# Squares as the stationary operand, byte-sign sums on VectorE and a polynomial inverse, in a macaron block on one core

## What is computed

```python
def ffn(x):                       # W_fc 512x128, W_proj 128x512
    y = square(relu(x @ W_fc.T)) @ W_proj.T
    mem = 0
    for _ in range(5):            # one input y, five steps
        reset = mem - 1 > 0
        mem = 0.9 * mem + y - reset
        spikes += mem - 1 > 0
    return spikes / 5
def attention(h):                 # per batch, down the 512 tokens
    keys, values = h @ Wk.T + bk, h @ Wv.T + bv
    w = exp((keys @ Wka.T + bka) / sqrt(128))
    w = w / cumsum(w, axis=1)
    return cumsum(w * keys, axis=1) * values
x = x + 0.5 * ffn(layernorm(x))
x = x + attention(layernorm(x) * gamma + beta)
x = x + 0.5 * ffn(layernorm(x))
```

## Time and profile before

| | us |
|---|---|
| median of 3 runs (156.86 to 157.18) | 157.02 |
| the profiled execution | 156.96 |
| its span, first to last instruction | 155.2 |
| PE matmul busy | 149.2 (96%) |
| DVE busy | 135.0 (87%) |
| ACT busy | 122.2 (79%) |
| POOL busy | 108.8 (70%) |

### The profile page before, as it was taken

The page is one execution under the profiler, slowest core; times in us unless marked ns, Lnnn a source line. Parts: engine busy times, 40 slices in busy tenths (PEclk is TensorE's granted clock), DMA queues, the critical chain, the costliest instruction groups (busy, mean ns, idle before and its releaser), DMA issues.

```text
span 155.2 us, 2591 instructions
## 1 busy us (share of the span) xinstructions
PE 149.2 (96%) x771; PEld 103.6 (67%) x771; DVE 135.0 (87%) x395; ACT 122.2 (79%) x238; POOL 108.8 (70%) x166
## 2 busy tenths in 40 slices
PE   6899999999999999999999999999999999999990
PEld 6684847585757848678566685785876848664790
DVE  2894589897999999999999999999999999965774
ACT  3286989899996985968989779498597685989871
POOL 1339128989699876899899999999987659080200
PEclk9999999999999999999999999999999999999999
DMA  4874000000000000000000020000020200211222
GB/s 158 231 196 143 0 2 4 0 0 2 0 2 4 2 0 0 0 4 0 0 0 0 0 72 2 0 0 0 2 72 0 68 0 1 67 44 30 68 68 70
DMA packets 10383, 5.08 MB, mean 33 GB/s; under 512 B 1153, under 2 KB 10241, under 8 KB 10369
## 3 DMA queue, kind: packets, MB, share of 16 engines
q1 hardware_dynamic: 9696, 4.40, 9.8%
q10 hardware_dynamic: 672, 0.52, 1.0%
HBM read 2.82 MB, written 2.10 MB: 32 GB/s over the span
## 4 chain that ended last, share of the span: by engine, by line
PE 93%; DVE 2%; DMA 2%; ACT 0%; issue 0%; SPq 0%; ACTq 0%
PE work L860 33%; PE hidden L796 10%; PE hidden L800 10%; PE hidden L797 9%; PE hidden L900 7%; PE work L809 5%; PE att_work L796 2%; PE att_work L800 2%; PE att_work L797 2%; PE att_work L909 2%; PE att_value L933 2%; DMA x_first<-_attn_hidden_states_dram 2%; PE att_value L796 1%; PE att_value L800 1%; PE att_value L797 1%; PE work L870 1%
## 5 line engine op out<-in xcount | busy, mean ns | idle before, releaser
L860 PE MATMUL work<-square,proj_t 128*128 128x512 f32 x120 | 58.0, 595 | 0.0
L415 ACT ACTIVATE relu<-hidden 128x512 f32<-128x512 f32 x64 | 39.7, 622 | 12.3 <-PE hidden L800 12.2
L448 ACT ACTIVATE signs<-work 128x512 bf16<-128x512 f32 x70 | 41.4, 612 | 7.2 <-PE work L860 7.2
L420 ACT ACTIVATE square<-relu 128x512 f32<-128x512 f32 x45 | 29.6, 657 | 0.6
L860 PEld LDWEIGHTS work<-square,proj_t 128*128 128x128 f32 x120 | 20.3, 189 | 12.7 <-issue 6.0
L672 DVE RECIPROCAL inv_sum<-weight_sum 128x256 f32<-128x256 f32 x16 | 27.9, 1741 | 0.0
L796 PE MATMUL hidden<-in_hi,fc_lo 128*128 128x512 f32 x64 | 27.1, 423 | 0.0
L343 POOL TENSOR_TENSOR rstd<-var_eps,minus_half 128x4 f32<-128x4 f32 x15 | 16.2, 1080 | 13.3 <-DVE neg_mean L529 13.3
L800 PE MATMUL hidden<-in_lo,fc_hi 128*128 128x512 f32 x64 | 25.2, 393 | 0.0
L797 PE MATMUL hidden<-in_hi,fc_hi 128*128 128x512 f32 x64 | 25.1, 392 | 0.0
L349 POOL TENSOR_SCALAR normed_att<-x_att,neg_mean_att,rstd_att 128x128 f32<-128x128 f32 x32 | 18.8, 600 | 0.8
(11 more groups left out here) (118 smaller groups left out, 265.5 us busy)
## 6 DMA issues: line engine op xcount, KB each, us to landing
x_first<-_attn_hidden_states_dram SPq DMA_DIRECT2D x7, 256.0 KB, 3.3
out_dram<-x_out SPq DMA_DIRECT2D x7, 256.0 KB, 2.2
fc_raw<-in_L_ffn_W_fc_dram ACTq DMA_DIRECT2D x1, 256.0 KB, 3.3
x_first<-_attn_hidden_states_dram SPq DMA_DIRECT2D x4, 64.0 KB, 3.0
proj_raw<-in_L_ffn_W_proj_dram ACTq DMA_DIRECT2D x1, 256.0 KB, 3.6
out_dram<-x_out SPq DMA_DIRECT2D x4, 64.0 KB, 1.5
att_raw<-in_L_attn_Wk_dram SPq DMA_DIRECT2D x1, 64.0 KB, 2.8
att_raw<-in_L_attn_Wv_dram SPq DMA_DIRECT2D x1, 64.0 KB, 2.5
```

The costliest lines, as they stand in the source:

```text
L415: nc.scalar.activation(relu[j.lane][:, c, :], hidden[c][:], ACT.Relu).then_inc(relu_made[j.lane], 1)
L420: nc.scalar.activation(square[j.lane][:, c, :], relu[j.lane][:, c, :], ACT.Square).then_inc(squares_act[j.lane], 1)
L448: nc.scalar.activation(signs[j.lane][:, k, :], work[j.lane][:], ACT.Sign, bias=bias, scale=scale).then_inc(signs_made[j.lane], 1)
L860: mm = nc.tensor.matmul(work[j.lane][:], proj_t[:, c, :], square[j.lane][:, c, :], start=(c == CONTRACT_ORDER[0]), stop=(c == CONTRACT_ORD ...
```

## The change

- **Contraction.** Every job is contracted as the last one was: for each chunk, four matmuls with a 128x128 tile of squares stationary and 128 columns of `proj_t` moving, into the same bank. The result has tokens on partitions. The counts (L900), their semaphore and the bf16 identity go.
- **Signs.** ACT writes the signs as bytes (0 or 1), for every job. DVE adds the planes by four adds over 256 words of 16 bits, now for attention jobs too, and the job's add reads the byte sum from SBUF.
- **Inverse.** In place of the reciprocal: ACT takes `guess` = exp(scale x bits + bias) of the running sum read as an integer, an estimate of its inverse. POOL multiplies `guess_sum` = sum x guess and `guess_share` = weight_key x guess. The rest is a cubic in guess_sum, as a linear factor by a quadratic one: ACT squares guess_sum off its centre into a PSUM bank `share_bank`, DVE adds `REST` and multiplies by guess_share (`att_near_share`), then multiplies by guess_sum - ROOT (`att_share_key`), both in that bank, and the scan reads it there. `weight_key` = (key + bias) x weight is made by DVE from `att_work`; ACT's key goes.
- **Banks.** `hidden` has three banks in rotation, and the one set free is `share_bank`.
- **Squares.** POOL squares no chunk of attention jobs; ACT does all four.
- **Layer norm.** `neg_mean` goes; the normalisation subtracts the mean from `moments`.
- **Order.** All four engines' lists are rearranged; the values are made in step i+1, the weight scan in step i.

```diff
-POOL_SQUARES = [(0,), (0,)]
-SIGN_ADDS = [4, 0]
 LAST_SQUARES = {"pool": (0,), "dve": (1, 2), "act": (3,)}
+POOL_SQUARES = [(0,), ()]
+SIGN_ADDS = [4, 4]
+POOL_SIGN_ADDS = [0, 0]
...
-        hidden = [bank(f"hidden{c}") for c in range(NC)]
-        count_bank = hidden[NC - 1]
+        hidden = [bank(f"hidden{n}") for n in range(HIDDEN_BANKS)]
+        share_bank = bank("share_bank")
         work = [bank(f"work{l}") for l in LANES]
         att_work, att_value = bank("att_work"), bank("att_value")
         first_second_half = hidden[1]
         last_lane = (len(FF_JOBS) - 1) % 2
-        y_tiles = [work[last_lane], att_work, att_value, hidden[0]]
+        y_tiles = [work[last_lane], att_work, att_value, share_bank]
...
+        def bank_of_hidden(j, c):
+            return hidden[(NC * j.index + c) % HIDDEN_BANKS]
...
-                cols = slice(half * HALF, (half + 1) * HALF)
-                pool.wait_ge(inv_made, 2 * b + half + 1)
-                if half == 0:
-                    pool.wait_ge(key_made, b + 1)
-                if b and half == 0:
-                    pool.wait_ge(pooled_made, b)
-                nc.gpsimd.tensor_tensor(share[:, cols], weight[b % ATT_SETS][:, cols], inv_sum[:, cols],
-                                        ALU.mult).then_inc(share_made, 1)
-                pool.wait_ge(share_made, 2 * b + half + 1)
-                nc.gpsimd.tensor_tensor(share_key[:, cols], share[:, cols], key[b % ATT_SETS][:, cols],
-                                        ALU.mult).then_inc(share_key_made, 1)
...
+            def att_guess_sum(b):
+                pool.wait_ge(guess_made, b + 1)
+                if b >= 2:
+                    pool.wait_ge(share_key_made, b - 1)
+                nc.gpsimd.tensor_tensor(guess_sum[b % 2][:], weight_sum[b % ATT_SETS][:], guess[b % 2][:],
+                                        ALU.mult).then_inc(guess_sum_made, 1)
+
+            def att_guess_share(b):
+                pool.wait_ge(guess_made, b + 1)
+                pool.wait_ge(weight_key_made, b + 1)
+                if b >= 2:
+                    pool.wait_ge(near_share_made, b - 1)
+                nc.gpsimd.tensor_tensor(guess_share[b % 2][:], weight_key[b % 2][:], guess[b % 2][:],
+                                        ALU.mult).then_inc(guess_share_made, 1)
...
             for i in range(FIRST_STEP, STEPS):
-                for b in attention(i - 1):
-                    att_shares(b, 0)
-                    att_shares(b, 1)
                 for j in feed_forward(i + 2):
                     ff_normalise(j)
-                for j in feed_forward(i + 1):
-                    ff_squares(j)
                 for b in attention(i + 2):
                     att_normalise(b)
+                for b in attention(i + 1):
+                    att_guess_sum(b)
+                    att_guess_share(b)
+                for j in feed_forward(i):
+                    ff_squares(j)
...
+                if b >= ATT_SETS:
+                    act.wait_ge(weight_key_made, b - ATT_SETS + 1)
+                    act.wait_ge(sum_made, b - ATT_SETS + 1)
                 nc.scalar.activation(weight[b % ATT_SETS][:], att_work[:], ACT.Exp, bias=exp_bias[:, 0:1],
                                      scale=KEY_SCALE).then_inc(weight_made, 1)
+
+            def att_guess(b):
+                act.wait_ge(sum_made, b + 1)
+                if b == 0:
+                    act.wait_ge(guess_consts_made, 2)
+                if b >= 2:
+                    act.wait_ge(guess_share_made, b - 1)
+                    act.wait_ge(guess_sum_made, b - 1)
+                nc.scalar.activation(guess[b % 2][:], weight_sum[b % ATT_SETS][:].bitcast(I32), ACT.Exp,
+                                     bias=log_bias[:, 0:1], scale=LOG_SCALE).then_inc(guess_made, 1)
+
+            def att_off_square(b):
+                act.wait_ge(guess_sum_made, b + 1)
+                if b:
+                    act.wait_ge(pooled_made, b)
+                nc.scalar.activation(share_bank[:], guess_sum[b % 2][:], ACT.Square,
+                                     bias=off_centre[:, 0:1]).then_inc(off_square_made, 1)
...
             for i in range(FIRST_STEP, STEPS):
+                for b in attention(i - 1):
+                    att_off_square(b)
                 for j in feed_forward(i - 1):
                     ff_sign(j, 0)
                     ff_sign(j, 1)
                 for j in feed_forward(i):
                     ff_relu(j, 0)
+                    ff_relu(j, 1)
+                    ff_square(j, 0)
                 for j in feed_forward(i - 1):
                     ff_sign(j, 2)
                 for b in attention(i):
                     att_weight(b)
                 for j in feed_forward(i):
-                    ff_relu(j, 1)
+                    ff_square(j, 1)
+                    ff_relu(j, 2)
                 for j in feed_forward(i - 1):
                     ff_sign(j, 3)
-                for j in feed_forward(i):
-                    ff_square(j, 1)
-                for b in attention(i):
-                    att_key(b)
-                for j in feed_forward(i):
-                    ff_relu(j, 2)
-                for j in feed_forward(i - 1):
                     ff_sign(j, 4)
                 for j in feed_forward(i):
                     ff_square(j, 2)
                     ff_relu(j, 3)
+                for b in attention(i):
+                    att_guess(b)
+                for j in feed_forward(i):
                     ff_square(j, 3)
                 for j in feed_forward(i + 1):
...
-                nc.vector.tensor_reduce(neg_mean[kind][:], moments[kind][:, :, 0:1], AXIS.X, ALU.add,
-                                        negate=True).then_inc(ln_args_made[kind], 1)
...
+                    nc.vector.tensor_tensor(sign_sum[j.lane][:].bitcast(U16), so_far.bitcast(U16),
+                                            signs[j.lane][:, k, :].bitcast(U16), ALU.add).then_inc(sign_sum_made[j.lane], 1)
 
             def ff_add(j):
                 if j.is_last:
                     return
 
-                dve.wait_ge(count_made[j.lane], j.turn + 1)
+                wait_sums(dve, j, j.sign_adds)
                 nc.vector.scalar_tensor_tensor(
-                    flat(x_of[NEXT[j.layer]][j.batch]), count_bank[:],
-                    RESIDUAL_STEP if j.by_pairs else RESIDUAL_STEP / 2,
+                    flat(x_of[NEXT[j.layer]][j.batch]), sign_sum[j.lane][:], RESIDUAL_STEP,
                     flat(x_of[j.layer][j.batch]), ALU.mult, ALU.add).then_inc(x_made[NEXT[j.layer]], 1)
...
-            def att_invert(b, half):
-                cols = slice(half * HALF, (half + 1) * HALF)
-                dve.wait_ge(sum_made, b + 1)
-                if b and half == 0:
-                    dve.wait_ge(share_made, 2 * b)
-                nc.vector.reciprocal(inv_sum[:, cols], weight_sum[b % ATT_SETS][:, cols]).then_inc(inv_made, 1)
+            def att_weight_key(b):
+                dve.wait_ge(key_mm, b + 1)
+                if b >= 2:
+                    dve.wait_ge(guess_share_made, b - 1)
+                nc.vector.scalar_tensor_tensor(weight_key[b % 2][:], att_work[:], kv_bias[:, 0:1],
+                                               weight[b % ATT_SETS][:], ALU.add,
+                                               ALU.mult).then_inc(weight_key_made, 1)
+
+            def att_near_share(b):
+                dve.wait_ge(off_square_made, b + 1)
+                dve.wait_ge(guess_share_made, b + 1)
+                nc.vector.scalar_tensor_tensor(share_bank[:], share_bank[:], REST, guess_share[b % 2][:],
+                                               ALU.add, ALU.mult).then_inc(near_share_made, 1)
+
+            def att_share_key(b):
+                dve.wait_ge(near_share_made, b + 1)
+                nc.vector.scalar_tensor_tensor(share_bank[:], guess_sum[b % 2][:], ROOT, share_bank[:],
+                                               ALU.subtract, ALU.mult).then_inc(share_key_made, 1)
 
             def att_pool(b):
-                dve.wait_ge(share_key_made, 2 * (b + 1))
-                nc.vector.tensor_tensor_scan(pooled[:], ones[:], share_key[:], 0.0, ALU.mult,
-                                             ALU.add).then_inc(pooled_made, 1)
+                dve.wait_ge(share_key_made, b + 1)
+                nc.vector.tensor_tensor_scan(pooled[:], ones[:], share_bank[:], 0.0, ALU.mult,
+                                             ALU.subtract).then_inc(pooled_made, 1)
...
             for i in range(FIRST_STEP, STEPS):
-                for j in feed_forward(i - 2):
-                    ff_sum_sign(j, 1)
-                    ff_sum_sign(j, 2)
-                for j in feed_forward(i - 1):
-                    ff_dve_square(j, 1)
-                    ff_dve_square(j, 2)
-                for b in attention(i - 2):
-                    att_invert(b, 0)
-                for b in attention(i - 1):
-                    att_sum(b)
```

(83 more changed lines are left out.)

206 lines of the change are left out of this document (112 added, 94 removed).

## The result

| | us |
|---|---|
| median of 4 runs (166.96 to 168.32), beside 157.1 of the kernel before | 167.19 |
| ratio to the kernel before, 95% interval | 1.064 (1.056 to 1.071) |
| the profiled execution / its span | 167.09 / 165.2 |

A forecast was written before the change was run, and what follows sets the result against it. PE was taken as the bound, with VectorE over it in steps 6, 9 and 10. Steps summed to 122.4 for 128.66, -6.3; span 148.9 plus 1.76 gave 150.7 us, range 148.4 to 154.0.

The forecast's parts named there:

- the part on POOL: POOL's work: squares, shares and share_key go, two products at 1.04 come; about 8 of 9.7 us in a full step.
- the 0.07 twice for neg_mean: VectorE's full step: removing neg_mean saves 0.07 us, twice.
- none of the four: Rivals: VectorE keeps up, chance 0.17; VectorE or ScalarE costs more, 0.25; port lock, 0.08; pieces save nothing, 0.04.
- Rival (c): VectorE's two-SBUF-input ops and POOL lock each other out; slower than before, about 159 us at 0.2 wait per op; chance 0.08.
- Counts gone: On PE, the count matmuls of all jobs disappear: -10.5 us.
- squares stationary: On PE, a job's contraction becomes 32 instructions of 0.112, 3.58 against 3.44 us, over 15 jobs: +2.1 us.
- the loop through ScalarE: Last contraction, ScalarE's signs, relus and squares, next last contraction: 7.3 us, so steps 1, 2 and 13 gain nothing.
- Steps 3 and 4: Pipeline steps forecast at 8.85 us (ScalarE's loop, PE's pieces 8.6) and 9.35 us (PE's pieces 9.3).
- VectorE's surplus over PE: VectorE exceeds PE by 0.9, 1.0 and 1.0 us in steps 6, 9 and 10; about half of 9 and 10's absorbed.
- VectorE's full step: VectorE's operations in steps 9 and 10 sum to 10.7 us, more than PE's 9.73.
- The sum of 16-bit words: VectorE's add over 256 words, without a row: taken as 0.25 us, four a step 1.0, bounds 0.85 and 1.4.
- the exponential of the integer view: ScalarE's guess, without a row: taken as 0.57 us from start to start, bounds 0.5 to 1.0.

The follow-up runs named there:

- the add restored: The changed kernel with VectorE making neg_mean again and POOL adding it in the normalisation, all else as changed: 152.94 us, ratio 0.974.
- moments and add: The changed kernel with POOL adding the mean column of moments instead of subtracting it, so normalised tiles are wrong: 151.86 us, ratio 0.968.
- the kernel without sums: The changed kernel with neg_mean and POOL's add back and the four sign sums of attention jobs left out, so those counts are wrong: 149.66 us.

## Why the prediction was wrong, point by point

**The step that failed is in the part on POOL, with the 0.07 twice for neg_mean beside it.** It costed the removal of neg_mean on VectorE, and took "about 8 of 9.7 us" for POOL's full step, with tiles at the old row's duration, although the diff changes the operation of that very instruction from add to subtract. Subtract-mult had no row; it was not named as a form without one, and got no bounds. It measured 0.80, 8 tiles a step: 8 x 0.35 = 2.8. The products add 0.5 (1.28 each for 1.04), which brings the 8 to 11.3, and the remaining 0.8 of the 12.1 goes with stretches beside VectorE (one tile of the period shown takes 1.67). Such stretches were in the old trace already, and the 8 has none: the kernel before has 9.6 us of unstretched work for POOL in a full step, and there POOL was busy for 10.3, 10.2 and 10.0 us of steps 9 to 11, which last 10.8; single tiles took up to 1.37. The 70% of the page was an average over stages. With bounds from 0.44 up, "POOL is the bound" would have been a rival; as it was, none of the four had POOL's own time as its mechanism.

**Rival (c), the slower one, named a mechanism that is real and was not the cause.** In the changed kernel a few sums take up to 1.03 for 0.29 (mean 407 ns over 42), 42 x 0.12 = 5 us of VectorE's time. With the add restored, and every such operation still in place, the mean is 323, the surplus 1.4 us, and the time 152.9: the waits grew where POOL no longer rested.

**The rest of the sum held, in groups of steps.** The forecast's steps beside those of the kernel with moments and add, whose VectorE and PE lists are those of the changed kernel (us between starts of turns):

| steps | before | forecast | moments and add | changed |
|---|---|---|---|---|
| 1, 2 | 14.6 | 14.7 | 14.5 | 15.8 |
| 3 to 6 | 37.2 | 36.3 | 36.6 | 41.2 |
| 7, 8 | 19.6 | 18.45 | 19.0 | 21.6 |
| 9 to 11 | 32.3 | 30.5 | 30.8 | 37.9 |
| 12 to 14 | 25.0 | 22.45 | 22.5 | 22.4 |

- Counts gone, squares stationary: right. A job's half contraction, 16 instructions, is 1.79 in the chain (0.112 each), and steps 9 to 11 of the kernel without sums are PE's sum to 0.03.
- Steps 1, 2 and 13 gain little, by the loop through ScalarE: right in sum; the ones measured are 7.47, 7.04 and 7.24. The recorded terms of that loop (5.6, 0.63, 0.1, 0.86, 0.2) add up to 7.39 and not to 7.3, so it found the 7.32 only to 0.1.
- Steps 3 and 4 last 9.04 and 9.71 for 8.85 and 9.35. They last 9.15 and 9.66 without the sums too, so it is not the sums; what holds them was not looked for.
- VectorE's surplus over PE was put into steps 9 and 10. It came in 10 and 11 (10.42 and 10.63, step 9 has 9.77), so that the sum 30.8 for 30.5 hides a shift by one step. The wait is the one that was named: weight_key ends at 105.83, and the attention turn of step 11 starts at 105.88.
- VectorE's full step, predicted 10.7: 96.24 to 106.87, 10.63, in these lines of the kernel with moments and add.

```profile
96.24 0.66 DVE L644 TENSOR_TENSOR in_lo<-work,in_hi 128x512 fp32r<-128x512 f32 x1
...
98.28 0.69 DVE L749 SCALAR_TENSOR_TENSOR share_bank<-share_bank,guess_share 128x512 f32<-128x512 f32 x1
98.88 0.68 DVE L729 SCALAR_TENSOR_TENSOR x_att<-sign_sum,x_first 128x512 f32<-128x512 uint8 x1
99.48 0.28 DVE L721 TENSOR_TENSOR sign_sum<-signs 128x256 uint16<-128x256 uint16 x1
99.69 0.86 DVE L583 BATCH_NORM_STATS2 stats_att<-x_att 128x6 f32<-128x128 f32 x4
...
106.87 0.66 DVE L644 TENSOR_TENSOR in_lo<-work,in_hi 128x512 fp32r<-128x512 f32 x1
```

  The sum of 16-bit words is 0.21 from start to start (taken: 0.25), the operation into a bank 0.60 (0.58).
- ScalarE: the exponential of the integer view has a duration of 0.80 and the square into a bank one of 0.69; from start to start they are 0.62 and 0.63 (step 4 of the same kernel), where 0.57 was taken in bounds of 0.5 to 1.0. Of the guesses without a row that the prediction did name none was far off.
- The changed kernel's PE also lost its clock twice: the clock row has a 7, an 8 and a 5 where it was full before. The granted clock is 0.50, the lower of the two levels (1.2 GHz), from about 96 to 100 us and from about 120.5 to 124, each time behind an attention turn in which PE waited some 0.45 us for each tile. In step 9 POOL's chain runs beside it. In step 11 PE is the chain: the 128-column contraction took 1.41 us for 8 instructions in place of 0.89 and five products 0.43 in place of 0.23. That is 0.5 + 1.0 = 1.5 us of the 14.3 and a consequence: with the add restored the clock is full.

```profile
120.34 1.41 PE work L949 x8
121.75 0.43 PE hidden L885
...
126.74 0.89 PE work L949 x8
```

## What to carry to other kernels

A row prices an instruction only with its operation, operands and engine; where a diff changes any of the three, however small it looks, the old duration is one bound and not the price. Ask that of every instruction that an engine repeats, above all on the engine that seems to have slack: here saving 0.07 us twice a step on VectorE cost 2.8 us a step on POOL. And slack is read in the step that counts, not on the page: POOL, at 70% of the span before, was at 93% to 95% in steps 9 to 11. When a step-by-step sum and the result differ wildly, compare the least duration of each line before and after: a changed least value is a changed instruction, a changed mean alone is company.

## What the runs showed of the hardware

- POOL's two-operation instruction with a subtract beside the multiply takes 0.80 us over 128 columns and 2.10 over 512, with an add 0.45 and 0.79. VectorE takes 0.34 over 128 columns for both, and POOL's add and subtract of two tensors of 512 columns 1.28 each.
- On POOL a product of two float32 tensors of 512 columns takes 1.28, of one with itself 1.06.
- A VectorE sum of 256 words of 16 bits with two SBUF inputs takes 0.28, and took 1.03 where it started 0.38 into a POOL product of 1.27.
